# A two-layer relational graph attention kernel: finding each block's row of codes with a matrix product, eight W1 tiles inside the block loop, and W1 products on three column groups

## The reference

```
xr = einsum('nd,rdf->rnf', x, W)            # 3 relations
oi, oj = xr[etype, dst], xr[etype, src]
alpha = leaky_relu(oi @ q + oj @ k, 0.2)
e = exp(alpha - segment_max(alpha, dst)[dst])
out = segment_sum(e / z[dst] * oj, dst) + b
h = elu(layer1(x)); y = layernorm(x + layer2(h))
```

## Time and profile before

| | us |
|---|---|
| median of 3 runs (1303.23 to 1304.97) | 1304.15 |
| the profiled execution | 1306.34 |
| its span | 1304.5 |
| busy: PE / PEld / DVE / ACT | 1258.2 / 1131.0 / 986.2 / 760.2 |
| the chain that ended last | PE 68%, DVE 21%, issue 4%, ACT 4%, DMA 3% |

### The profile page before, as it was taken

One profiled execution on the slowest core, in us unless ns is written; L12 is line 12 of the kernel. 1 busy time (PEld: TensorE's weight loads), 2 busy tenths in 40 slices (PEclk: granted clock), 3 DMA queues, 4 the chain that ended last, 5 costly groups with the idle time before them and its releaser, 6 DMA issues.

```text
span 1304.5 us, 18701 instructions
## 1 busy us (share of the span) xinstructions
PE 1258.2 (96%) x7086; PEld 1131.0 (87%) x7086; DVE 986.2 (76%) x1280; ACT 760.2 (58%) x1212; POOL 6.7 (1%) x21
## 2 busy tenths in 40 slices
PE   6999999998899999999999999999989999999996
PEld 5666656665689999999999999999989999999995
DVE  1389899999399989989989976768835456656554
ACT  3566633322199979979979953247544443564462
POOL 1000000000000000000000000000000000000000
PEclk9999999999899999999999999999989999999998
DMA  9420131111354313323333227954387765778860
GB/s 328 162 94 26 37 127 49 43 49 49 135 129 133 102 49 111 117 77 101 102 96 97 62 79 232 301 184 166 127 306 264 248 232 205 262 265 308 282 231 34
DMA packets 93815, 195.77 MB, mean 150 GB/s; under 512 B 15997, under 2 KB 66270, under 8 KB 93730
## 3 DMA queue, kind: packets, MB, share of 16 engines
q1 hardware_dynamic: 93408, 193.77, 44.5%
q0 software_dynamic: 224, 0.68, 0.2%
q10 hardware_dynamic: 98, 0.16, 0.0%
HBM read 154.73 MB, written 39.85 MB: 149 GB/s over the span
## 4 chain that ended last, share of the span: by engine, by line
PE 68%; DVE 21%; issue 4%; ACT 4%; DMA 3%; SPq 1%; ACTq 0%; DVEq 0%
PE ps L1157 23%; PE ps L1115 23%; PE ps L968 10%; DVE arena L1296 9%; PE ps L943 4%; PE ps L1025 3%; PE ps L916 2%; DVE arena L1353 2%; DMA arena<-in_L_gnn_W 2%; DVE arena L1357 1%; ACT arena L707 1%; DVE misc L1306 1%; PE ps L901 1%; DVE ps L1425 1%; ACT arena L708 1%
## 5 line engine op out<-in xcount | busy, mean ns | idle before, releaser
L1115 PE MATMUL ps<-arena 128*128 128x193 f32 x2400 | 397.0, 327 | 3.0 <-DVE arena L1357 2.7
L1115 PEld LDWEIGHTS ps<-arena 128*128 128x128 f32 x2400 | 392.1, 190 | 5.7 <-DVE arena L1357 5.1
L943 PE MATMUL ps<-arena,xT 128*128 128x384 f32 (+1 forms) x720 | 250.7, 493 | 0.0
L707 ACT ACTIVATE arena<-arena,misc 128x640 f32<-128x640 f32 x240 | 197.2, 822 | 31.4 <-DVE arena L1353 23.4
L708 ACT ACTIVATE arena<-arena,misc 128x640 f32<-128x640 f32 x240 | 196.0, 817 | 0.0
L1353 DVE TENSOR_TENSOR arena<-arena 128x1280 f32<-128x1280 f32 x120 | 178.3, 1486 | 22.6 <-ACT arena L708 22.4
L943 PEld LDWEIGHTS ps<-arena,xT 128*128 128x128 f32 x720 | 130.3, 190 | 73.2
L1357 DVE SCALAR_TENSOR_TENSOR arena<-arena,Ct 128x1280 f32<-128x1280 f32 x120 | 179.2, 1493 | 14.0 <-DVE arena L1353 9.9
L1296 DVE SCALAR_TENSOR_TENSOR arena<-arena,misc 128x1250 f32<-128x1250 bf16 x108 | 155.6, 1513 | 0.0
L824 ACT ACTIVATE g_hi<-arena 128x512 fp32r<-128x512 f32 (+2 forms) x90 | 49.7, 552 | 159.0 <-PE ps L1157 143.5
L1157 PE MATMUL ps<-x2a,g_hi 128*128 128x384 f32 (+1 forms) x600 | 131.8, 342 | 4.3 <-issue 4.3
(11 more groups left out here) (170 smaller groups left out, 1376.2 us busy)
## 6 DMA issues: line engine op xcount, KB each, us to landing
x2a<-xr_d SPq DMA_DIRECT2D x45, 776.0 KB, 4.3
x2b<-xr_d SPq DMA_DIRECT2D x45, 776.0 KB, 4.5
arena<-xr_d SPq DMA_DIRECT2D x120, 193.0 KB, 2.4
xr_d<-stg SPq DMA_DIRECT2D x60, 384.0 KB, 3.0
arena<-ab_d SPq DMA_DIRECT2D x12, 1280.0 KB, 6.4
xr_d<-bb SPq DMA_DIRECT2D x60, 193.0 KB, 2.2
arena<-in_L_gnn_W SPq DMA_DIRECT2D x5, 2304.0 KB, 9.8
arena<-in_L_gnn_W SPq DMA_DIRECT2D x7, 1152.0 KB, 6.8
```

What stands on the lines that cost most here:

```text
L707: nc.scalar.activation(weights1(g, r, t)[:, h, :], abr[:, r, h, :], ACT.Exp, bias=qk1t[:, t, col + R * H:col + R * H + 1])
L943: last = mm(unit1_bank(u)[:, 0:w], xT[:, kt, t * P:(t + 1) * P], v, start=kt == 0, stop=kt == KT - 1)
L1115: last = mm(bank1(g, i)[:, o:o + HD + 1], weights1(g, r, t)[:, h, i * P:(i + 1) * P], xring[t % NX][:, o:o + HD + 1], start=False, stop=Tr ...
```

## The change

- The two-level search loses its row gather. VectorE casts the destinations to float (`dstf`, 500 columns and one more with 500 * partition). Two tiny DMAs bring each row's neighbours' first destinations (`ends`). From these VectorE makes G, which is 1 only in the one row in which a block's start lies. Two products G x dstf (80 rows, 112 columns of G, 501 columns of dstf) put that row and its base offset in PSUM, where VectorE counts.
- The run transposes move ahead: behind the fifth group of x transposes, in bank 2. All four casts to bf16 are VectorE's.
- W1 tiles 10 to 17 move into the block loop: transposes of tile 10 + i behind pair 3i, its product behind pair 3i + 3. The units start at pair 27, and 10 instead of 12 lie in the loop.
- The six matmuls of a W1 product go to three groups of output partitions (0, 32, 64), two each. The copy takes 72 partitions, and the transposes become matmuls with `qsum`, a 0/1 matrix that adds the three groups.

```diff
@@ search
-rowb = cut(rowb_at, 2 * EC)...
+dstf = cut(pos[0], EC + 1)
+ends = smalli[:, 5:7].bitcast(I32)
 SP:
+sp.wait_ge(S["ends_set"], 2)
+first = dst.rearrange("(p c) -> p c", p=EP)[1:EP, 0:1]
+sp.dma_start(ends[1:EP, 0:1], first, ...)
+sp.dma_start(ends[0:EP - 1, 1:2], first, ...)
 POOL:
-pool.wait_ge(S["row_ready"], 1)
-for s in range(2):
-    nc.gpsimd.indirect_dma_start(rowb[0:SG, s, :], ...)
 PE, ahead of the first tile:
+pe.wait_ge(S["ranks"], 1)
+for s in range(2):
+    last = mm(ps[s][0:SG, 0:EC + 1], G[0:EP, s * SW:s * SW + SG], dstf[0:EP, :], start=True, stop=True)
-    last = mm(ps[1][0:SG, s:s + 1], G[...], onesf[0:EP, 0:1], ...)      # was at tile 2
 DVE:
+V.tensor_scalar(small[:, 2:4], small[:, 0:2], float(WIN), None, ALU.mult)
+V.tensor_copy(dstf[0:EP, 0:EC], dsti[0:EP, :])
+V.tensor_copy(small[0:EP, 4:6], ends[0:EP, :])
+link(V.tensor_scalar(Gn[0:EP, :], wrow[0:EP, :], small[0:EP, 5:6], None, ALU.is_gt))
+V.scalar_tensor_tensor(G[0:EP, :], wrow[0:EP, :], small[0:EP, 4:5], Gn[0:EP, :], ALU.is_gt, ALU.subtract)
-dve.wait_ge(S["rows_in"], 32)
-    link(V.tensor_scalar(tmpf[0:SG, :], rowb[0:SG, s, :], ...
+    link(V.tensor_scalar(tmpf[0:SG, :], ps[s][0:SG, 0:EC], ...
@@ where the tiles and units stand
+PRE = 10
+WT_AT = {3 * (i - PRE): i for i in range(PRE, R * KT)}
+WQ_AT = {p + 3: i for p, i in WT_AT.items()}
+WQ_END = max(WQ_AT) + 1
+T_AT = WQ_END + 2
-NL = 12
+NL = NT
-RUNS_AT = 11
+RUNS_AT = 4
 def steps0(pair):
-    return range(max(0, NK0 * pair // PAIRS), max(0, NK0 * (pair + 1) // PAIRS))
+    n = PAIRS - T_AT
+    return range(max(0, NK0 * (pair - T_AT) // n), max(0, NK0 * (pair + 1 - T_AT) // n))
@@ PE, in the block loop (ACT has wt_out, wq_out, wq_columns behind the copy of the pair after)
+if pair in WT_AT:
+    wt_transposes(WT_AT[pair])
+if pair in WQ_AT:
+    wq_product(WQ_AT[pair])
+if pair == WQ_END:
+    wq_transposes(R - 1)
@@ products
-    last = mm(ps[6 + kt // 3][0:2 * H, ...], qv1[:, ft, :], WT[i % 2][...], start=ft == 0, stop=ft == KT - 1)
+    q = 32 * (ft % NQ)
+    last = mm(ps[6 + kt // 3][q:q + 2 * H, ...], qv1[:, ft, :], WT[i % 2][...], start=ft < NQ, stop=ft >= KT - NQ)
-    last = nc.tensor.transpose(ps[7][...], wqs[0:2 * H, kt * P:(kt + 1) * P], ident[0:2 * H, 0:2 * H])
+    last = mm(ps[7][...], wqs[0:QP, kt * P:(kt + 1) * P], qsum[0:QP, :], start=True, stop=True)
@@ casts: the two of slo_2 from ACT (at tile 14) to DVE
```

More of the change, by code:

```diff
@@ L137, in rgat @@
         small = sb("small", [P, 64])
+        qsum_t = sb("qsum", [P, 2 * H])
         smalli = sb("smalli", [P, 8], U32)
@@ L154, in rgat @@
         NE = 2 * RUN * SW
+        NWR = SW + SG
         NB = max(NE, EC)
@@ L164, in rgat @@
         f0, f1, wid, slo, mcode = (v[:, 0:NE] for v in (f0_, f1_, wid_, slo_, mcode_))
-        wrow = take(SW + SG)
-        G = take(SW + SG)
+        wrow = take(NWR)
+        G = take(NWR)
+        Gn = u1_[:, 0:NWR]
         slo_2 = cut(rowb_at, NE).bitcast(BF16).rearrange("p (n a) -> p n a", a=2)
@@ L176, in rgat @@
         wqs = take(F)
+        NQ = 3
+        QP = 32 * (NQ - 1) + 2 * H
+        ends = smalli[:, 5:7].bitcast(I32)
+        qsum = qsum_t[:, :]
         B0_AT = ARENA - KT * (HF + QC)
@@ L405, in _ @@
                 sp.dma_start(t[0:EP, :], a.rearrange("(p c) -> p c", p=EP)).then_inc(S["edges_in"], 16)
+            sp.wait_ge(S["ends_set"], 2)
+            first = dst.rearrange("(p c) -> p c", p=EP)[1:EP, 0:1]
+            sp.dma_start(ends[1:EP, 0:1], first, allow_slow_non_contiguous=True).then_inc(S["ends_in"], 16)
+            sp.dma_start(ends[0:EP - 1, 1:2], first, allow_slow_non_contiguous=True).then_inc(S["ends_in"], 16)
             sp.dma_start(qv1[:, :, 0:H], q1.rearrange("(k p) h -> p k h", p=P), allow_slow_non_contiguous=True).then_inc(S["qv_in"], 16)
@@ L610, in wq_out @@
                     for b in range(2):
-                        last = nc.scalar.activation(wqs[0:2 * H, b * HF:(b + 1) * HF], ps[6 + b][0:2 * H, 0:HF], copy)
+                        last = nc.scalar.activation(wqs[0:QP, b * HF:(b + 1) * HF], ps[6 + b][0:QP, 0:HF], copy)
                     last.then_inc(S["wqs_ready"], 1)
@@ L666, in _ @@
                     wq_out(KT - 1)
-            for i in range(KT, R * KT):
+            for i in range(KT, PRE):
                 wt_out(i)
@@ L670, in _ @@
                     wq_out(i - 2)
[L671 to L677, removed]
+            for i in range(PRE - 2, PRE):
                 wq_out(i)
-            wq_columns(R - 1)
             act.sem_inc(S["c_ready"], 2)
@@ L685, in _ @@
                                      ps[pair % 2][:, 0:2 * WM].rearrange("p (c a b) -> p a c b", c=2, b=WIN), copy).then_inc(S["c_ready"], 1)
+                if pair - 1 in WT_AT:
+                    wt_out(WT_AT[pair - 1])
+                if pair - 1 in WQ_AT:
+                    wq_out(WQ_AT[pair - 1])
+                if pair - 1 == WQ_END:
+                    wq_columns(R - 1)
                 for n in steps0(pair - 1):
@@ L695, in ab_rows @@
                 last.then_inc(S["ab_rows"], 1)
-            for u in range(NK0 * (PAIRS - 1) // PAIRS // KT, NL):
+            for u in range(NK0 * (PAIRS - 1 - T_AT) // (PAIRS - T_AT) // KT, NL):
                 transform_out(u)
@@ L910, in wq_product @@
                     pe.wait_ge(S["qv_in"], 32)
+                    pe.wait_ge(S["wq_zero"], 2)
                 if r and kt == 0:
@@ L915, in wq_product @@
                 for ft in range(KT):
-                    last = mm(ps[6 + kt // 3][0:2 * H, kt % 3 * P:(kt % 3 + 1) * P], qv1[:, ft, :], WT[i % 2][:, ft * P:(ft + 1) * P],
-                              start=ft == 0, stop=ft == KT - 1)
+                    q = 32 * (ft % NQ)
+                    last = mm(ps[6 + kt // 3][q:q + 2 * H, kt % 3 * P:(kt % 3 + 1) * P], qv1[:, ft, :], WT[i % 2][:, ft * P:(ft + 1) * P],
+                              start=ft < NQ, stop=ft >= KT - NQ)
                 last.then_inc(S["wq_done"], 1)
@@ L924, in wq_transposes @@
                 pe.wait_ge(S["wqs_ready"], r + 1)
+                if r == 0:
+                    pe.wait_ge(S["qsum_ready"], 2)
                 for kt in range(KT):
-                    last = nc.tensor.transpose(ps[7][:, HF + kt * 2 * H:HF + (kt + 1) * 2 * H], wqs[0:2 * H, kt * P:(kt + 1) * P], ident[0:2 * H, 0:2 * H])
+                    last = mm(ps[7][:, HF + kt * 2 * H:HF + (kt + 1) * 2 * H], wqs[0:QP, kt * P:(kt + 1) * P], qsum[0:QP, :], start=True, stop=True)
                 last.then_inc(S["wq_tr"], 1)
@@ L969, in unit @@
                 last.then_inc(S["t_done"], 1)
+            pe.wait_ge(S["ranks"], 1)
+            for s in range(2):
+                last = mm(ps[s][0:SG, 0:EC + 1], G[0:EP, s * SW:s * SW + SG], dstf[0:EP, :], start=True, stop=True)
+            last.then_inc(S["ranks"], 1)
             for i in range(KT):
[L973 to L977, removed]
                 wt_transposes(i)
@@ L998, in _ @@
                         wq_product(KT - 2 + kt // 2)
[L999 to L1007, removed]
+                    if t0 == 0 and kt == RUNS_AT:
+                        pe.wait_ge(S["runs_in"], 32)
+                        for s in range(2):
+                            for t_ in range(RUN):
+                                c = (s * RUN + t_) * SW
+                                last = nc.tensor.transpose(ps[2][:, c:c + SW], runb[0:SW, s, t_ * P:(t_ + 1) * P], ident[0:SW, 0:SW])
+                        last.then_inc(S["run_tr"], 1)
+            for i in range(KT, PRE):
                 wt_transposes(i)
@@ L1010, in _ @@
                     wq_product(i - 2)
-            for i in range(R * KT - 2, R * KT):
+            for i in range(PRE - 2, PRE):
                 wq_product(i)
-            wq_transposes(R - 1)
             pe.sem_inc(S["c_done"], 2)
@@ L1173, in link @@
                 dve.wait_ge(S["chain"], links[0])
+            V.memset(ends[0:EP, 0:1], -1).then_inc(S["ends_set"], 1)
+            V.memset(ends[0:EP, 1:2], N).then_inc(S["ends_set"], 1)
             V.memset(x_sb[:, NT - 1, :], 0.0).then_inc(S["x_zero"], 1)
@@ L1177, in _ @@
             links[0] += 1
+            for b in range(2):
+                V.memset(ps[6 + b][0:QP, 0:HF], 0.0).then_inc(S["wq_zero"], 1)
             dve.wait_ge(S["edges_in"], 48)
@@ L1182, in _ @@
             dve.sem_inc(S["code_ready"], 1)
[L1184 to L1187, removed]
+            dve.wait_ge(S["consts"], 9)
+            V.tensor_tensor(qsum, ident[:, 0:2 * H], ident[:, 32:32 + 2 * H], ALU.add).then_inc(S["qsum_ready"], 1)
@@ new lines, in _ @@
+            dve.wait_ge(S["ends_in"], 32)
+            V.tensor_scalar(small[:, 2:4], small[:, 0:2], float(WIN), None, ALU.mult).then_inc(S["chain"], 1)
+            V.tensor_copy(dstf[0:EP, 0:EC], dsti[0:EP, :]).then_inc(S["chain"], 1)
+            V.tensor_copy(small[0:EP, 4:6], ends[0:EP, :]).then_inc(S["chain"], 1)
+            links[0] += 3
+            dve.wait_ge(S["chain"], links[0])
```

(18 more changed lines are left out.)

28 lines of the change are left out of this document (11 added, 17 removed).

## The result

The changed kernel takes 1292.66 us (median of four, 1290.11 to 1294.57), the kernel before 1304.49: ratio 0.9911, interval 0.9894 to 0.9928, 11.8 us faster. In a later set beside other kernels it was 1294.28 against 1303.82 (0.9920, 0.9906 to 0.9934). The profiled execution took 1294.57 us with a span of 1292.6. The forecast was 1294.6, and the direction and nearly the size came out. That the size is so near is partly luck: some of its terms were wrong in opposite directions.

The account below looks back on a forecast made before the run. TensorE was taken to bound everything to the block loop's end: loop start 40.8 us instead of 64.97, loop 14.6 longer, so end 9.5 earlier; 0 behind it. 1304.15 - 9.5 = 1294.6 us, range 1287 to 1304.

Parts of the forecast that it names:

- The bound: Up to the block loop's end at 149 us TensorE bounds the kernel; then VectorE's maxima, whose start sets the end.
- The product: Twelve matmul records of a W1 tile: 0.85 us instead of 1.41, bounds 0.47 and 1.41.
- rival 1: The column groups overlap more: a product takes 0.6 us, the kernel 1290 us; chance 0.20.
- the prediction's own sign: The forecast is wrong if, among other signs, a W1 product misses 0.7 to 1.0 us.
- Rival 3: No overlap, and the array empties on entering and leaving grouped mode: 1.72 us a product, 1310 us; chance 0.07.
- Setup: TensorE's work ahead of the block loop: the loop starts at about 40.8 us instead of 64.97.
- The qsum matmuls: The wqs transposes as twelve fp32 records: 1.7 us against 0.53, bounds 1.4 and 2.3.
- Groups of three: First pairs of the loop, carrying eight W1 tiles: 3.11 us a group, its fourth pair waiting for ScalarE's copy.
- The other 79 pairs: Rest of the block loop, with 60 unit steps: 79 x 0.315 + 60 x 0.715 = 67.8 us.
- Behind the loop: Two units move there: maxima 1.3 us late, about 1.3 back as the clock holds; sum 0, bounds -2 and +3.

Follow-up runs that it names:

- e1: The changed kernel with the six matmuls of each W1 product on one column group again: 1304.68 us, ratio 1.0004 to the kernel before.
- e12: The changed kernel with two column groups instead of three: 1295.05 us in one execution, a product 0.76 us.
- e5: The changed kernel with the two small loads issued from ACT's queue and the rank products between tiles 1 and 2: 1291.31 us, ratio 0.9906.
- e2: The kernel before with the three column groups alone and what they need (zeroed banks, wider copy, qsum matmuls): 1297.52 us, ratio 0.9939.
- e8: The changed kernel with each product in the loop one pair later, apart from the next tile's transposes: 1290.37 us, ratio 0.9892.
- e6: The changed kernel with ACT's masks due one tile earlier (lag 3 instead of 2): 1292.21 us, ratio 0.9905.
- e7: The kernel before with the three column groups and ten units in the loop, without the search and the tiles in the loop: 1295.35 us, ratio 0.9934.
- e3: The changed kernel with W1 tiles 10 to 17 ahead of the loop again, the ten units spread over all 106 pairs: 1294.72 us, ratio 0.9921.
- e9: The changed kernel with the edits of e5, e6 and e8 together: 1288.46 us, ratio 0.9878.
- e4: The kernel before with ten instead of twelve units in the loop, nothing else: 1301.16 us, ratio 0.9980.
- e11: The changed kernel unaltered, run again in the same rounds as e9: 1294.28 us.

## Why the prediction was right, and where it was not

- **The bound** was read rightly: TensorE's work up to the end of the block loop. e1 shows it. Giving back 18 x 0.86 us of work there gives back the whole gain.
- **The product** was mis-sized: 0.85 forecast, 0.55 measured. I had let only neighbours of different groups overlap. e12 shows that the groups run fully side by side. This is what rival 1 says (0.6 us), and it was worth 18 x 0.3 = 5.4 us. By the prediction's own sign (wrong if the product misses 0.7 to 1.0 us) this step failed; that the time came out at the forecast is owed to what follows. Rival 3's emptying at each change of mode is at most 0.08 us a product. The Trainium skill ("TensorE: Matmul & The Clock Gate", Part 3) gives 2.38 times for three column tiles at 512 columns; here, with 128 columns in fp32, it is 1.41 / 0.55 = 2.6.
- **Setup** ate three of those microseconds. SP's extra issues cost 1.5 us, not 0.95: W1's first issue is at 4.71 instead of 3.19. The rank products end at 11.1 us, not 9.9. W1[1] landed at 33.06 us, not 28.5. I had taken the median of two loads (16.8 us) for this one, which took 21.07. The trace of the kernel before, asked for 10 to 13 us alone, has the right number, and all other traces have 20.1 to 22.5:

```profile
arena<-in_L_gnn_W SPq DMA_DIRECT2D x1, 2304.0 KB, 22.4
```

To this come 3.58 us for 18 transposes at a granted clock that fell to 0.50. The start at 41.0 against my 40.8 is such a balance. e5 shows that the wait for W1[1] can be avoided.
- **The qsum matmuls** took 1.44 us, inside the bounds, near the 1.7 taken. In e2 they took 2.45 in the second seam, at a granted clock of 0.50.
- **Groups of three** took 2.75 us, where I had 3.11: the product's 0.30 less, and 0.06. (3.11 is 0.5 above TensorE's own 2.61, not the 0.7 that I wrote; the sum doesn't use it.) The mechanism, the copy behind a long stretch, is shown by e8.
- **The other 79 pairs** took 69.3 us (68.8 to 138.1), where I had 67.8. 1.7 us of it is the fall of the clock at 70 us; without it the term is right. The prediction expected such a fall only behind long idle and looked at the clock only at the closing transposes. By the same rows the groups alone (e2) lost 3.0 us to it.
- **Behind the loop** the sum was right by chance. Forecast: a wait of 1.3 us for transposes at the end of relation 1, and 1.3 back from the clock. Measured: no such wait; 1.49 us for a mask that stands in ACT's queue behind a unit's copy, of which the prediction says nothing; and 1.7 us back (329.32 to 340.95 us is 11.63, 319.93 to 329.83 is 9.90). e6 shows both: when the mask's wait is taken away, the forecast wait appears, with 0.41 us of the 1.3.
- **What each part is worth**: ten units 2.9, the column groups 6.5, both 8.9, all with search and tiles in the loop 9.5 to 11.8. The search does nothing alone that these runs can tell (e7 against e3). What it allows, tiles in the loop, adds 0.4 to 2 us, within the noise. The three edits of e9 add 5.8: they take out waits that came with the search (the small loads), with the ten units (the mask, which e4 has too) and with the tiles in the loop (product beside transposes).

Open: what makes TensorE slow in its first microseconds; why W1[1]'s wait lowers the clock in one execution and not in another (in e11, the same kernel, tile 6 waits 1.86 us and the stretch of 33 to 34 us reads 1.00); and how much of the gain would come back if the clock held behind the last product.

## What to carry to other kernels

Where one engine bounds a long stretch, moving its work about within the stretch gains only the waits at the seams; taking work off it gains more, until the loads and copies that it had hidden come due (here a load at 33 us and the copy behind a long stretch). With less work between the same waits TensorE's granted clock can fall as well: read it in stretches of 1 us at each seam, since a mean over the run (0.991 before, 0.992 after) doesn't show it. Small stationary operands of 8 columns are such work: spread over three column groups, an accumulation took 0.55 us instead of 1.41. Long pieces of work put into a loop should stand apart from each other, by at least the latency of the copy that the next iteration waits for.

## What was not expected of the hardware

- fp32 matmuls with 8-column operands run side by side on three column groups, both records of each: 0.046 us a record against 0.117.
- TensorE's first 12 transposes take 0.21 us each instead of 0.11, and its 501-column fp32 records 0.83 us instead of 0.44, with a granted clock of 1.00 in the rows. This lasted to 11 us in e5 and to 14.6 us in the changed kernel.
- A wait of 1.73 us, behind a stretch with many short waits, was enough for the granted clock to read 0.50 for some 3 us in one execution; 1.85 us of idle at 320 us, behind dense work, was not. A wait of 1.31 us, behind products on three groups, was followed by 3 to 7 us at 0.50; 1.29 us behind products on one group (e1) was not.
